# Wide probability tiles of an attention kernel normalised on ScalarE in place of VectorE

## The chip, the cores and the metric

One core of a Trainium2 chip runs the whole program. The metric is the device time of one execution in microseconds (us), lower is better. The kernel is written instruction by instruction: every engine has its own program, and the engines meet only at semaphores.

## The reference

A transformer block on 8 sequences of 512 tokens, width 512: attention with a residual, then a mixture of experts with a residual. The attention has 16 query heads in 4 groups that share a key and value head, and adds two parts, softmax attention and a gated linear recurrence. Cut to what matters here:

```python
qs = softmax(q, axis=-1)                      # "features", over the head's 128 columns
ks = softmax(k, axis=-1)
gl = log_sigmoid(g) / 16.0                    # g is k
S  = S * exp(gl_t)[..., None] + ks_t[..., None] * v_t[..., None, :]     # scan over tokens
o_gla = einsum('bhk,bhkv->bhv', qs_t, S)
scores = einsum('bqhd,bkhd->bhqk', rope(q), rope(k)) * D ** -0.5        # causal mask
attn = softmax(scores, axis=-1)
y = einsum('bhqk,bkhd->bqhd', attn, v)
out = (0.5 * y + 0.5 * o_gla) @ Wo
```

## The kernel before, in words

The program has three phases: attention, routing with the shared expert, and the 32 experts. The change touches the attention alone.

Attention works in *units*, one for each sequence and group, 8 x 4 = 32, and a first one that only prepares. A unit (`unit(c, b, g, prepare, more)`, one such function in the program of every engine) does two things side by side. It attends the four query heads of its group, and, where `prepare` is set (31 of the 32), it prepares the next unit: the query, key and value products, the rotary embedding, the softmax features, the gates, for four blocks of 128 tokens. Head s and block s share a *head step*, s = 0 to 3, so that each unit has three switches from one head to the next.

A head's scores are cut by query rows into four tiles i = 0 to 3 of 128 rows; the causal mask leaves tile i with 128 (i + 1) columns. "The fourth tile" is i = 3 (512 columns), "the third" i = 2 (384 columns): the wide ones. Each goes this way:

- TensorE, `scores` (L781, L783): the scores into `score_ps`.
- VectorE, `row_max` (L583), then ScalarE, `exponent` (L412): the exponential into `prob[:, i % 2]`, with its row sums.
- VectorE, `normalise`: the reciprocal of the row sums (L589, it counts up `inv_sum_ready`) and the multiplication in place (L591, it counts up `prob_ready`).
- TensorE, `turn_probs` (L797): waits for `prob_ready` and transposes the tile block by block. For the third tile it also waits for `o_whole_ready`, since it writes into `out_ps`, which ScalarE must have emptied.
- VectorE, `diagonal` (L599), adds the recurrence's local part to the last block; ScalarE, `past` (L418), copies the other blocks to `prob_t`.
- TensorE, `attend` (L808, L811): the products into `out_ps`. ScalarE, `out_copy` (L424, L428), empties it, GpSimd makes the low half of the output.

The features of block s: ScalarE `take_products` (L437 to L440) brings them from PSUM; VectorE `feature_max` (L605) and `rope_cosines` (L613); ScalarE `gates` (L445, L447) and `feature_exps` (five exponentials of 128 columns with row sums, L454); VectorE `gate_logs` (L619) and `soften_keys` (reciprocal L625, multiplication L627, which counts up `soft_key_ready`). In the next head step TensorE's `turn_features` (L874 and on) waits for that count and transposes, then `turn_queries` (L888), and after more products `turn_softmax` (L895). ScalarE's `turned_keys` and `turned`, VectorE's `turned_low` (L634), `apply_decays` and `keep_local` (L665), and GpSimd's functions go on from there.

In group 2 of a sequence that has a successor, each head step also turns a part of the next input: ScalarE `turned_x` (L397) behind the feature exponentials, VectorE `x_low` (L565), and `turn_queries` waits for it. In group 1 VectorE takes that input's statistics.

The order on each engine is the order in which its `unit` calls these functions; nothing is rescheduled. At a switch, ScalarE exponentiates the next head's wide tiles before `gates`, and VectorE normalises them between `keep_local` and `gate_logs`:

```python
                    if c is not None and s < G - 1:      # VectorE
                        normalise(c, s + 1, 3)
                        normalise(c, s + 1, 2)
                    if prepare:
                        gate_logs(NT * ua + s)
                        soften_keys(NT * ua + s)
```

The first head's wide tiles are normalised at the start of the unit, ahead of the steps, while TensorE runs the first query and value products.

Of the kernel before, what the change touches and what calls it, by code (L numbers as in the profile page):

```python
# [6 lines left out]
P = 128  # L7
# [6 lines left out]
ACT = mybir.ActivationFunctionType  # L14
# [6 lines left out]
G = HEADS // KV  # L21
# [3 lines left out]
NT = SEQ // P  # L25
# [16 lines left out]
def attention_phase(nc, x, w_q, w_k, w_v, w_o, consts, x2, acc, rows):  # L42
# [3 lines left out]
    with ExitStack() as ctx:  # L46
        def sb(name, shape, dt=F32):
            return ctx.enter_context(nc.sbuf_tensor(name, shape, dt))

        def sem(name):  # L50
            return ctx.enter_context(nc.semaphore(name))
# [40 lines left out]
        prob = sb("prob", [P, 2, SEQ])  # L92
# [3 lines left out]
        inv_sum = sb("inv_sum", [P, G * NT])  # L96
# [67 lines left out]
        exp_ready = [sem(f"exp_ready{n}") for n in range(2)]  # L164
        inv_sum_ready = sem("inv_sum_ready")
        prob_ready = sem("prob_ready")
        prob_turned = [sem(f"prob_turned{n}") for n in range(2)]
        past_copied = sem("past_copied")
        diag_ready = sem("diag_ready")
# [49 lines left out]
        def block_index(c, h, i):  # L219
            return G * NT * c + NT * h + NT - 1 - i  # L220

        def use_index(c, h, i):

            return G * NT // 2 * c + NT // 2 * h + (NT - 1 - i) // 2
# [152 lines left out]
        def _(act):  # L377
# [30 lines left out]
            def exponent(c, h, i):  # L408
                n, k, j, w = block_index(c, h, i), use_index(c, h, i), NT * h + i, P * (i + 1)
                act.wait_ge(max_ready, n + 1)  # L410
                act.wait_ge(prob_turned[i % 2], k)
                nc.scalar.activation(prob[:, i % 2, 0:w], score_ps[i % 2][:, 0:w], ACT.Exp, bias=neg_max[:, j:j + 1],  # L412
                                     accum_out=row_sum[:, j:j + 1]).then_inc(exp_ready[i % 2], 1)

            def past(c, h, i):
                act.wait_ge(diag_ready, block_index(c, h, i) + 1)
                act.wait_ge(attended, G * c + h)
                nc.scalar.copy(prob_t[:, 0:i, i * P:(i + 1) * P],  # L418
                               prob_ps[i % 2][:, 0:i * P].rearrange("p (j t) -> p j t", t=P)).then_inc(past_copied, 1)
# [22 lines left out]
            def gates(a):  # L442

                act.wait_ge(logs_step, 3 * a + 1)
                nc.scalar.activation(logs[:], logs[:], ACT.Exp, scale=-1.0).then_inc(logs_step, 1)  # L445
                act.wait_ge(logs_step, 3 * a + 2)
                nc.scalar.activation(logs[:], logs[:], ACT.Ln, bias=1.0).then_inc(logs_step, 1)  # L447

            def feature_exps(a, ua, i):
                act.wait_ge(tops_ready, a + 1)  # L450
                act.wait_ge(soft_turned, a)
                act.wait_ge(k_rest_ready, (NT - 1) * ua + min(i, NT - 1))
                for h in range(G + 1):
                    ins = nc.scalar.activation(soft[:, h * DH:(h + 1) * DH], qk[:, h * DH:(h + 1) * DH], ACT.Exp,  # L454
                                               bias=neg_top[:, h:h + 1], accum_out=tot[:, h:h + 1])
                ins.then_inc(exps_ready, 1)
# [19 lines left out]
            def unit(c, b, g, prepare, more):  # L476
                ua, p = (0, 0) if c is None else (c + 1, (g + 1) % 2)
                if prepare and c is not None:
                    act.wait_ge(attended, G * c)
                if c is not None:  # L480
                    exponent(c, 0, 3)
                    exponent(c, 0, 2)
                for s in range(NT):
                    if c is not None:
                        past(c, s, 3)
                        exponent(c, s, 1)
                    if prepare and s:
                        turned_keys(NT * ua + s - 1, p, s - 1)
                    if c is not None:
                        past(c, s, 2)  # L490
                        exponent(c, s, 0)
                    if prepare and s:
                        turned(NT * ua + s - 1, ua, p, s - 1)
                    if prepare:
                        take_products(NT * ua + s, p, s)
                    if c is not None:
                        if s < G - 1:
                            exponent(c, s + 1, 3)
                        past(c, s, 1)
                        if s < G - 1:  # L500
                            exponent(c, s + 1, 2)
                    if prepare:
                        gates(NT * ua + s)
                        feature_exps(NT * ua + s, ua, s)
                    if more and g == KV - 2:
                        turned_x(b + 1, s, tr_ps[min(s, 1)])
                    if c is not None:
                        out_copy(c, s, NT * ua + s if prepare else None)
                    else:
                        split_high(STAGES + s)  # L510
                if prepare:
                    turned_keys(NT * ua + NT - 1, p, NT - 1)
                    turned(NT * ua + NT - 1, ua, p, NT - 1)
                if more and g == KV - 3:
                    root(b + 1)
                if c is None:
                    act.wait_ge(w_low, STAGES + DC)
            each_sequence(act, head, unit)

        @block.vector  # L520
        def _(dve):
# [64 lines left out]
            def normalise(c, h, i):  # L586
                n, j, w = block_index(c, h, i), NT * h + i, P * (i + 1)
                dve.wait_ge(exp_ready[i % 2], use_index(c, h, i) + 1)
                nc.vector.reciprocal(inv_sum[:, j:j + 1], row_sum[:, j:j + 1]).then_inc(inv_sum_ready, 1)  # L589
                dve.wait_ge(inv_sum_ready, n + 1)  # L590
                nc.vector.tensor_scalar(prob[:, i % 2, 0:w], prob[:, i % 2, 0:w], inv_sum[:, j:j + 1], None,  # L591
                                        ALU.mult).then_inc(prob_ready, 1)
# [152 lines left out]
        def _(pe):  # L745
# [38 lines left out]
                                 stop=True).then_inc(scores_done, 1)  # L784

            def turn_probs(c, h, i):
                n = block_index(c, h, i)
                pe.wait_ge(prob_ready, n + 1)
                if i == NT - 1 and h == 0:
                    pe.wait_ge(x2_added[1], NT // 2 * c)  # L790
                if i == 2:
                    pe.wait_ge(o_whole_ready, G * c + h)
                else:

                    pe.wait_ge(past_copied, (NT - 1) * (G * c + h) + max(NT - 2 - i, 0))
                for j in range(i + 1):
                    ins = nc.tensor.transpose(prob_ps[i % 2][:, j * P:(j + 1) * P], prob[:, i % 2, j * P:(j + 1) * P], ident[:])  # L797
                ins.then_inc(prob_turned[i % 2], 1)
# [1236 lines left out]
```

## Time and profile before

| | |
|---|---|
| three runs | 2785.82, 2787.27, 2788.97 us |
| their median | 2787.27 us |
| the profiled execution's own time | 2786.35 us |
| its span, first to last instruction | 2784.3 us |
| mean granted TensorE clock over the span | 0.974 |

All durations come from the profiled execution. Its span leaves out the 2.05 us around the first and last instruction. In the rows "PE" is TensorE's matmul, "PEld" its weight load, which overlaps the matmuls, "DVE" VectorE, "ACT" ScalarE, "POOL" GpSimd, "SP" the engine that issues transfers. A row of a timeline has the start in us from the span's beginning, the duration in us, engine, line of the kernel, operation, output<-input with partitions x elements, and in brackets the idle time of the engine before it with what ended it ("issue": nothing that the profile shows). Neighbours on an engine overlap a little. The granted clock is 1.00 at TensorE's full 2.4 GHz.

### The profile page before, as it was taken

Reading aid. Unit: us, or ns where it says so; the run is one execution under the profiler, and the core shown is the slowest. Engines: PE = TensorE matmul, PEld = TensorE weight load, DVE = VectorE, ACT = ScalarE, POOL = GpSimd, SP = SyncE. Lnnn points to the kernel's source line nnn. Section 1 sums busy time; section 2 is a strip of 40 time slices with the busy share of each in tenths; the row PEclk is TensorE's granted clock in tenths of the full one; section 3 lists DMA queues with packets and bytes.
Section 4 is the critical chain, followed back from the end, with each engine's and each line's share of the span. In section 5 each row is a group of like instructions: output and inputs, shape, how many; then the busy total and the mean of one; then the engine's idle time right before and its main releaser. Section 6 shows DMA issues by size and latency. Waiting matters only on the chain. (4 is left out here: it accounts for less than half of the span.)

```text
span 2784.3 us, 52836 instructions
## 1 busy us (share of the span) xinstructions
PE 2533.7 (91%) x16740; PEld 1726.4 (62%) x16740; DVE 1912.5 (69%) x4603; ACT 1571.3 (56%) x4783; POOL 1563.6 (56%) x2010
## 2 busy tenths in 40 slices
PE   3899999999999999999999999999986899979882
PEld 2566666666666666666666666666654345457661
DVE  5777767777777776777677767777756677647661
ACT  4666556666665666666566655666644243146661
POOL 3556545655665565566556555655531666646563
PEclk9899999999999999999999999999998999989996
DMA  4500000000000000000000000000003314159985
GB/s 174 191 1 16 1 31 1 16 31 1 2 16 31 1 16 29 4 1 17 31 1 1 16 31 1 1 31 1 1 1 115 113 52 148 63 153 260 272 224 149
DMA packets 65358, 156.80 MB, mean 56 GB/s; under 512 B 13367, under 2 KB 14647, under 8 KB 64256
## 3 DMA queue, kind: packets, MB, share of 16 engines
q1 hardware_dynamic: 48624, 132.91, 14.0%
q0 software_dynamic: 16384, 16.33, 3.2%
q10 hardware_dynamic: 80, 4.19, 0.4%
q8 instruction: 141, 2.31, 0.3%
q14 instruction: 129, 1.06, 0.1%
HBM read 120.31 MB, written 81.40 MB: 72 GB/s over the span
## 5 line engine op out<-in xcount | busy, mean ns | idle before, releaser
L284 POOL TENSOR_TENSOR parts<-qk,rope 128x640 f32<-128x640 f32 x128 | 197.0, 1539 | 451.6 <-issue 303.4
L412 ACT ACTIVATE prob<-score_ps,neg_max 128x512 f32<-128x512 f32 (+3 forms) x512 | 271.8, 531 | 249.8 <-DVE neg_max L583 213.5
L808 PE MATMUL out_ps<-prob_t,val 128*128 128x512 f32 (+3 forms) x1024 | 309.0, 445 | 14.3 <-ACT prob_t L418 10.3
L781 PE MATMUL score_ps<-kr_t,qr_t 128*128 128x512 f16 (+3 forms) x1536 | 284.8, 300 | 13.2 <-ACT prob L412 11.4
L591 DVE TENSOR_SCALAR prob<-prob,inv_sum 128x512 f32<-128x512 f32 (+3 forms) x512 | 272.9, 533 | 18.0
L808 PEld LDWEIGHTS out_ps<-prob_t,val 128*128 128x128 f32 x1024 | 186.7, 192 | 135.8 <-issue 64.3
L583 DVE TENSOR_REDUCE neg_max<-score_ps 128x1 f32<-128x512 f32 (+3 forms) x512 | 237.5, 483 | 26.2 <-PE score_ps L783 20.1
L454 ACT ACTIVATE soft<-qk,neg_top 128x128 f32<-128x128 f32 x640 | 247.1, 387 | 0.8
L324 POOL TENSOR_TENSOR k_dec<-decay,keys 128x32 f32<-128x32 f32 (+3 forms) x512 | 165.0, 354 | 83.1 <-ACT decay L474 83.1
L854 PE MATMUL qkv_ps<-wq_high,x_t_high 128*128 128x512 f16 x512 | 197.0, 385 | 15.8 <-DVE wkv_low L531 15.8
L296 POOL TENSOR_TENSOR rot<-parts 128x320 f32<-128x320 f32 x128 | 110.6, 864 | 168.0 <-DVE parts L613 168.0
L589 DVE RECIPROCAL inv_sum<-row_sum 128x1 f32<-128x1 f32 x512 | 81.4, 159 | 174.4 <-ACT prob L412 174.2
L854 PE MATMUL qkv_ps<-wq_low,x_t_high 128*128 128x512 f16 x512 | 196.3, 383 | 0.0
L854 PE MATMUL qkv_ps<-wq_high,x_t_low 128*128 128x512 f16 x512 | 195.8, 382 | 0.0
L337 POOL TENSOR_TENSOR o_t_low<-parts,o_t_high 128x512 f16<-128x512 f32 x128 | 148.0, 1156 | 77.3 <-ACT parts L428 77.3
L781 PEld LDWEIGHTS score_ps<-kr_t,qr_t 128*128 128x128 f16 x1536 | 135.7, 98 | 83.0 <-ACT prob L412 38.5
L302 POOL TENSOR_TENSOR soft<-soft,inv_tot 128x512 f32<-128x512 f32 x128 | 145.9, 1140 | 63.4 <-DVE inv_tot L625 63.4
L437 ACT ACTIVATE qk<-qkv_ps 128x640 f32<-128x640 f32 x128 | 90.0, 703 | 152.8 <-issue 138.1
L1799 POOL DMA_INDIRECT acc<-e_yo,e_goal x64 | 115.1, 1799 | 106.1 <-issue 88.9
L418 ACT COPY prob_t<-prob_ps 128x384 f32<-128x384 f32 (+1 forms) x256 | 94.3, 368 | 118.0 <-DVE prob_t L599 116.4
L1257 POOL DMA_INDIRECT rows<-r_yn,r_sk_i x128 | 129.0, 1008 | 53.9 <-issue 47.3
L313 POOL TENSOR_TENSOR decay<-keys 128x512 f32<-128x512 f32 x128 | 142.5, 1113 | 6.2 <-ACT keys L461 4.2
(285 smaller groups left out, 7780.0 us busy)
## 6 DMA issues: line engine op xcount, KB each, us to landing
held_expert_w<-in_L_ffn_W_gate_dram SPq DMA_DIRECT2D x32, 512.0 KB
held_expert_w<-in_L_ffn_W_up_dram SPq DMA_DIRECT2D x32, 512.0 KB
held_expert_w<-in_L_ffn_W_down_dram SPq DMA_DIRECT2D x32, 512.0 KB, 7.2
rows<-const_empty_dram SPq DMA_DIRECT2D x1, 10560.0 KB, 39.2
e_xg<-rows SPq DMA_DIRECT2D x32, 330.0 KB
x_in<-_attn_hidden_states_dram SPq DMA_DIRECT2D x8, 1024.0 KB, 5.4
x_acc<-_attn_hidden_states_dram SPq DMA_DIRECT2D x8, 1024.0 KB, 5.4
x<-x_acc SPq DMA_DIRECT2D x8, 1024.0 KB, 4.4
```

Source lines behind the costliest of these rows:

```text
L284: nc.gpsimd.tensor_tensor(parts[:, 1, :].rearrange("p (h d) -> p h d", d=HALF), qk[:].rearrange("p (h d) -> p h d", d=HALF), rope[:, i, 1: ...
L302: nc.gpsimd.tensor_tensor(q, q, inv_tot[:, 0:G].unsqueeze(2).to_broadcast([P, G, DH]), ALU.mult).then_inc(soft_query_ready, 1)
L313: nc.gpsimd.tensor_tensor(decay[:, 0:NSUB * P].rearrange("p (c s) -> p c s", s=P), mid.to_broadcast([P, NSUB, P]), run.unsqueeze(1).to_bro ...
L324: ins = nc.gpsimd.tensor_tensor(k_dec[:, s, 0:m], decay[:, s * P:s * P + m], keys[:, 0:m], ALU.mult)
L337: nc.gpsimd.tensor_tensor(o_t[1][:, h, :], o_whole, o_t[0][:, h, :], ALU.subtract).then_inc(o_t_ready, 1)
L412: nc.scalar.activation(prob[:, i % 2, 0:w], score_ps[i % 2][:, 0:w], ACT.Exp, bias=neg_max[:, j:j + 1], accum_out=row_sum[:, j:j + 1]).the ...
L454: ins = nc.scalar.activation(soft[:, h * DH:(h + 1) * DH], qk[:, h * DH:(h + 1) * DH], ACT.Exp, bias=neg_top[:, h:h + 1], accum_out=tot[:, ...
L583: nc.vector.tensor_reduce(neg_max[:, j:j + 1], score_ps[i % 2][:, 0:w], AX_X, ALU.max, negate=True).then_inc(max_ready, 1)
L591: nc.vector.tensor_scalar(prob[:, i % 2, 0:w], prob[:, i % 2, 0:w], inv_sum[:, j:j + 1], None, ALU.mult).then_inc(prob_ready, 1)
L781: nc.tensor.matmul(score_ps[i % 2][:, 0:w], qr_t[p][:, q_, h, i * P:(i + 1) * P], kr_t[p][:, k_, 0:w], start=(n == 0), stop=False)
L808: nc.tensor.matmul(out_ps[:, j * P:SEQ], val[p][:, j, :], prob_t[:, j, j * P:SEQ], start=(j == 0), stop=False, skip_group_check=True)
L854: ins = nc.tensor.matmul(qkv_ps[:, 0:G * DH], x_t[x_part][:, d, i * P:(i + 1) * P], wq[w][:, d, gn * G * DH:(gn + 1) * G * DH], start=(d = ...
```

## The change

The two wide tiles of each head are no longer multiplied by VectorE but by ScalarE, with a Copy whose scale is the column of reciprocals (`normalise_wide`). VectorE still takes all reciprocals and multiplies the two narrow tiles. ScalarE does the fourth tile's Copy after `gates` and ahead of `feature_exps`, and the third tile's behind `feature_exps`; at a unit's start both come behind the two exponentials. The wide Copies count up a semaphore of their own, `wide_prob_ready`, for which TensorE's transposes of those tiles wait; both counts are taken per head, two for each. The instructions of TensorE, GpSimd and the transfers stay as they are, in the same order.

```diff
--- before.py
+++ after.py
@@ -164,6 +164,7 @@
         exp_ready = [sem(f"exp_ready{n}") for n in range(2)]
         inv_sum_ready = sem("inv_sum_ready")
         prob_ready = sem("prob_ready")
+        wide_prob_ready = sem("wide_prob_ready")
         prob_turned = [sem(f"prob_turned{n}") for n in range(2)]
         past_copied = sem("past_copied")
         diag_ready = sem("diag_ready")
@@ -412,6 +413,12 @@
                 nc.scalar.activation(prob[:, i % 2, 0:w], score_ps[i % 2][:, 0:w], ACT.Exp, bias=neg_max[:, j:j + 1],
                                      accum_out=row_sum[:, j:j + 1]).then_inc(exp_ready[i % 2], 1)
 
+            def normalise_wide(c, h, i):
+                n, j, w = block_index(c, h, i), NT * h + i, P * (i + 1)
+                act.wait_ge(inv_sum_ready, n + 1)
+                nc.scalar.activation(prob[:, i % 2, 0:w], prob[:, i % 2, 0:w], ACT.Copy,
+                                     scale=inv_sum[:, j:j + 1]).then_inc(wide_prob_ready, 1)
+
             def past(c, h, i):
                 act.wait_ge(diag_ready, block_index(c, h, i) + 1)
                 act.wait_ge(attended, G * c + h)
@@ -480,6 +487,8 @@
                 if c is not None:
                     exponent(c, 0, 3)
                     exponent(c, 0, 2)
+                    normalise_wide(c, 0, 3)
+                    normalise_wide(c, 0, 2)
                 for s in range(NT):
                     if c is not None:
                         past(c, s, 3)
@@ -501,7 +510,12 @@
                             exponent(c, s + 1, 2)
                     if prepare:
                         gates(NT * ua + s)
+                    if c is not None and s < G - 1:
+                        normalise_wide(c, s + 1, 3)
+                    if prepare:
                         feature_exps(NT * ua + s, ua, s)
+                    if c is not None and s < G - 1:
+                        normalise_wide(c, s + 1, 2)
                     if more and g == KV - 2:
                         turned_x(b + 1, s, tr_ps[min(s, 1)])
                     if c is not None:
@@ -587,6 +601,8 @@
                 n, j, w = block_index(c, h, i), NT * h + i, P * (i + 1)
                 dve.wait_ge(exp_ready[i % 2], use_index(c, h, i) + 1)
                 nc.vector.reciprocal(inv_sum[:, j:j + 1], row_sum[:, j:j + 1]).then_inc(inv_sum_ready, 1)
+                if i >= 2:
+                    return
                 dve.wait_ge(inv_sum_ready, n + 1)
                 nc.vector.tensor_scalar(prob[:, i % 2, 0:w], prob[:, i % 2, 0:w], inv_sum[:, j:j + 1], None,
                                         ALU.mult).then_inc(prob_ready, 1)
@@ -784,8 +800,10 @@
                                  stop=True).then_inc(scores_done, 1)
 
             def turn_probs(c, h, i):
-                n = block_index(c, h, i)
-                pe.wait_ge(prob_ready, n + 1)
+                if i >= 2:
+                    pe.wait_ge(wide_prob_ready, 2 * (G * c + h) + NT - i)
+                else:
+                    pe.wait_ge(prob_ready, 2 * (G * c + h) + 2 - i)
                 if i == NT - 1 and h == 0:
                     pe.wait_ge(x2_added[1], NT // 2 * c)
                 if i == 2:
```

How the order moves at a switch, on ScalarE, before (from the next head's third tile's exponential to the two copies of this head's output; `tot` are the row sums):

```order
L412 ACTIVATE prob,row_sum<-score_ps,neg_max 128x384 [waits prob_turned0,max_ready]
L445 ACTIVATE logs<-logs 128x128 [waits logs_step]
L447 ACTIVATE logs<-logs 128x128 [waits logs_step]
L454 ACTIVATE soft,tot<-qk,neg_top 128x128 [waits k_rest_ready,soft_turned,tops_ready]
L454 ACTIVATE soft,tot<-qk,neg_top 128x128 x4
L424 ACTIVATE o_t_high<-out_ps 128x512 [waits projected,attended]
L428 ACTIVATE parts<-out_ps 128x512 [waits rot_ready,o_t_ready]
```

and with the change, where L413 is the same exponential, L419 the new Copy, L461 the feature exponentials, L431 and L435 the output copies:

```order
L413 ACTIVATE prob,row_sum<-score_ps,neg_max 128x384 [waits prob_turned0,max_ready]
L452 ACTIVATE logs<-logs 128x128 [waits logs_step]
L454 ACTIVATE logs<-logs 128x128 [waits logs_step]
L419 ACTIVATE prob<-prob,inv_sum 128x512 [waits inv_sum_ready]
L461 ACTIVATE soft,tot<-qk,neg_top 128x128 [waits k_rest_ready,soft_turned,tops_ready]
L461 ACTIVATE soft,tot<-qk,neg_top 128x128 x4
L419 ACTIVATE prob<-prob,inv_sum 128x384 [waits inv_sum_ready]
L431 ACTIVATE o_t_high<-out_ps 128x512 [waits projected,attended]
L435 ACTIVATE parts<-out_ps 128x512 [waits rot_ready,o_t_ready]
```

Two Copies have come in, one on either side of the five feature exponentials; each waits for `inv_sum_ready`, which VectorE counts up.

VectorE at the first switch of a unit, before (from the rotary cosines to the softened keys):

```order
L613 TENSOR_TENSOR parts<-qk,rope 128x640 [waits rot_ready,o_t_ready]
L589 RECIPROCAL inv_sum<-row_sum 128x1 [waits exp_ready1]
L591 TENSOR_SCALAR prob<-prob,inv_sum 128x512 [waits inv_sum_ready]
L589 RECIPROCAL inv_sum<-row_sum 128x1 [waits exp_ready0]
L591 TENSOR_SCALAR prob<-prob,inv_sum 128x384 [waits inv_sum_ready]
L619 SCALAR_TENSOR_TENSOR gate<-qk,logs 128x128 [waits keys_turned,logs_step]
L625 RECIPROCAL inv_tot<-tot 128x5 [waits soft_query_ready,exps_ready]
L627 TENSOR_TENSOR soft<-soft,inv_tot 128x128 [waits inv_ready]
```

and with the change (L603 the reciprocals of the row sums, L635 the gate, L641 and L643 the keys):

```order
L629 TENSOR_TENSOR parts<-qk,rope 128x640 [waits rot_ready,o_t_ready]
L603 RECIPROCAL inv_sum<-row_sum 128x1 [waits exp_ready1]
L603 RECIPROCAL inv_sum<-row_sum 128x1 [waits exp_ready0]
L635 SCALAR_TENSOR_TENSOR gate<-qk,logs 128x128 [waits keys_turned,logs_step]
L641 RECIPROCAL inv_tot<-tot 128x5 [waits soft_query_ready,exps_ready]
L643 TENSOR_TENSOR soft<-soft,inv_tot 128x128 [waits inv_ready]
```

The two multiplications by `inv_sum` are gone; the two reciprocals stand next to each other, still behind what was ahead of them. At the later switches `keep_local` (L665) stands between the cosines and the reciprocals, in both kernels.

## Rows read from the trace of the kernel before

**Rows 1.** Busy time, share of the span and instructions of each engine, whole program.
```profile
PE 2533.7 (91%) x16740; PEld 1726.4 (62%) x16740; DVE 1912.5 (69%) x4603; ACT 1571.3 (56%) x4783; POOL 1563.6 (56%) x2010
```

**Rows 2.** Busy us by engine (instructions), clock, DMA share, GB/s, 64 us of attention.
```profile
1000.00:1064.00 64.00, 63.24 (x414) 43.73 (x413) 45.97 (x116) 41.44 (x141) 38.89 (x50) 1.00 0.06 18
```

**Rows 3.** Waits of TensorE: engine, line, releaser: us in total, times, longest.
```profile
PE tr_ps L874 <- DVE soft L627: 32.7, 79, 5.2
...
PEld tr_ps L874 <- issue: 33.1, 83, 0.5
```

**Rows 4.** Timeline of TensorE's weight loads, one head step.
```profile
1194.20 0.14 PEld L874 LDWEIGHTS tr_ps<-ident,rot 128*128 128x128 f32 x1 [0.38 <-issue]
...
1207.25 0.14 PEld L874 LDWEIGHTS tr_ps<-ident,rot 128*128 128x128 f32 x1 [0.37 <-issue]
...
1208.30 0.36 PEld L797 LDWEIGHTS out_ps<-ident,prob 128*128 128x128 f32 x3
```

**Rows 5.** Timeline of VectorE in the same head step.
```profile
1201.38 1.16 DVE L583 TENSOR_REDUCE neg_max<-score_ps 128x1 f32<-128x512 f32 x2 [0.36 <-PE score_ps L783]
...
1204.91 0.15 DVE L589 RECIPROCAL inv_sum<-row_sum 128x1 f32<-128x1 f32 x1
1205.09 0.52 DVE L591 TENSOR_SCALAR prob<-prob,inv_sum 128x512 f32<-128x512 f32 x1
...
1205.72 0.83 DVE L591 TENSOR_SCALAR prob<-prob,inv_sum 128x384 f32<-128x384 f32 x1
...
1206.67 0.18 DVE L625 RECIPROCAL inv_tot<-tot 128x5 f32<-128x5 f32 x1
1206.89 0.29 DVE L627 TENSOR_TENSOR soft<-soft,inv_tot 128x128 f32<-128x128 f32 x1
```

**Rows 6.** Timeline of ScalarE in the same head step.
```profile
1204.16 0.39 ACT L454 ACTIVATE soft<-qk,neg_top 128x128 f32<-128x128 f32 x1
...
1205.99 0.19 ACT L454 ACTIVATION_READ_ACCUMULATOR soft<-qk,neg_top 128x1 f32 x1
1206.32 0.60 ACT L424 ACTIVATE o_t_high<-out_ps 128x512 f16<-128x512 f32 x1
1206.82 0.59 ACT L428 ACTIVATE parts<-out_ps 128x512 f32<-128x512 f32 x1
```

**Rows 7.** ScalarE groups by shape: busy us, mean ns of one, idle before.
```profile
L418 ACT COPY prob_t<-prob_ps 128x384 f32<-128x384 f32 x128 | 61.3, 479 | 112.5 <-DVE prob_t L599 110.9
...
L1840 ACT ACTIVATE e_yo<-e_down_ps,e_share 80x512 f32<-80x512 f32 x64 | 40.8, 678 | 87.1 <-POOL e_goal L1790 79.2 <-PE e_down_ps L1940 5.7 <-DMA acc<-e_yo,e_goal 2.1
...
L1295 ACT ACTIVATE r_yn<-r_xr,r_shift,r_rstd 128x512 f32<-128x512 f32 x32 | 23.4, 805 | 7.5 <-DVE r_shift L1513 7.5
L1328 ACT CAST r_h_high<-r_h 128x512 f16<-128x512 f32 x32 | 20.2, 630 | 60.6 <-DVE r_h L1623 57.8 <-issue 2.8
```

**Rows 8.** Timeline, first switch of a group 0: ScalarE and TensorE's weight load.
```profile
1371.33 0.60 ACT L424 ACTIVATE o_t_high<-out_ps 128x512 f16<-128x512 f32 x1 [1.83 <-PE out_ps L811]
...
1371.89 0.14 PEld L874 LDWEIGHTS tr_ps<-ident,rot 128*128 128x128 f32 x1
```

**Rows 9.** Timeline, a group 2 switch, with the next input's turn.
```profile
1001.71 0.15 DVE L589 RECIPROCAL inv_sum<-row_sum 128x1 f32<-128x1 f32 x1
...
1002.89 0.58 ACT L397 ACTIVATE x_t_high<-tr_ps 128x512 f16<-128x512 f32 x1
...
1003.90 0.68 DVE L565 SCALAR_TENSOR_TENSOR x_t_low<-tr_ps,x_t_high 128x512 f16<-128x512 f32 x1
...
1004.67 0.48 PEld L888 LDWEIGHTS tr_ps<-ident,rot 128*128 128x128 f32 x4
```

**Rows 10.** Timeline, starts of a group 2 and of a group 3 unit.
```profile
1231.95 0.20 ACT L412 ACTIVATION_READ_ACCUMULATOR prob<-score_ps,neg_max 128x1 f32 x1
...
1232.80 0.47 PEld L797 LDWEIGHTS prob_ps<-ident,prob 128*128 128x128 f32 x4
...
1294.40 0.42 DVE L591 TENSOR_SCALAR prob<-prob,inv_sum 128x384 f32<-128x384 f32 x1
```

## The prediction

> **What bounds the kernel now.** I read the page first. TensorE is busy for 91% of the span, ScalarE for 56%, VectorE for 69% [rows 1]. That says where to look and not what the change is worth, so the stage comes next: 64 us of attention in the middle of the program hold 63.24 us of matmuls at a granted clock of 1.00 [rows 2]. TensorE is the bound there, and only work that makes TensorE wait can move the time. The waits in front of it are small and tell what stands close behind. The first transpose of a block's features, L874, waits for the softened keys of VectorE's L627 (32.7 us in 79 waits), and its weight load for 33.1 us in 83 more waits that end in "issue" [rows 3]. These are two views of one stop and not two sums.
>
> The timeline of one head step shows the chain behind it. The same transpose starts at 1194.20 and at 1207.25, so a step takes 13.05 us [rows 4]. The second one comes behind 0.37 us of idle. On VectorE, from the two row maxima at 1201.38 to L627 at 1206.89, one instruction follows the other with no idle [rows 5]. L627 ends at 1207.18 and L874 starts 0.07 later. Ahead of it ScalarE's five feature exponentials (L454) run from 1204.16 to 1206.18, the end of their last accumulator read [rows 6]; they are done 0.49 us before VectorE turns to them at 1206.67. So VectorE's chain decides by half a microsecond, and ScalarE's is next.
>
> **The change, part by part.**
>
> *Removed from VectorE.* In a head step the two wide multiplications stand at 1205.09 (0.52) and 1205.72 (0.83) [rows 5]. Taking both out frees about 1.2 us between the first reciprocal and the gate. If nothing else followed, the transpose would lose its 0.37 us wait and no more, since TensorE has its own work up to there. That is the most that can be won.
>
> *Added to ScalarE, and its cost.* No row shows this operation (Copy, SBUF to SBUF, scale from a column). From below: the 128x512 cast from SBUF with no column operand takes 630 ns. From above: L1295, SBUF to SBUF with two column operands, takes 805 ns. One column costs about 0.09 us by L1840, 678 ns, against L428, the same width without a column, 0.59 [rows 6, 7]; so I take 0.71 us for the fourth tile. L418 with 384 elements takes 479 ns, 0.11 less than L428 with 512, so 0.60 for the third. Neighbours on ScalarE start about 0.10 us before the end of the one ahead (1206.32 and 0.60, next at 1206.82 [rows 6]), so they hold the queue for 0.61 and 0.50. The Trainium skill, "ScalarE: Activation LUTs", section "What ACT_TABLE_LOAD costs", gives 186 + 93 + 0.833 x 512 = 706 ns as an estimate for it; the sum would be the same.
>
> *The new wait.* ScalarE now stops behind L447 until VectorE has written the reciprocal. That reciprocal is still behind L665, at 1204.91 [rows 5], and the next VectorE instruction uses it 0.19 later, so ScalarE can start at 1205.10. Before, the exponentials started at 1204.16. Queued behind the waiting instruction are the exponentials, then the third tile's Copy, then both copies of the head's output.
>
> *The sum for a step.* Exponentials start at 1205.10 + 0.61 = 1205.71, 1.55 later than before. Their last read ends 2.02 later at 1207.73. VectorE, which has been idle, takes the reciprocal (L625) at 1207.77; L627 follows 0.22 later for 0.29 us and ends at 1208.28; L874 starts at 1208.35 instead of 1207.25. **TensorE loses 1.10 us in the step**. All that follows in the step hangs on TensorE: the next row maxima wait 0.36 us for L783 [rows 5], so nothing catches up.
>
> *How many steps.* 8 sequences of 4 groups are 32 units, of which 31 prepare the next one; each has three switches from one head to the next, 93. At the first switch of a group 0 the transpose (1371.89) has no wait in front and ScalarE idles 1.83 us for the output at 1371.33 [rows 8]: 1.0 us later is hidden there, in 8 units. That leaves 85 steps: 85 x 1.10 = 93.5 us.
>
> *Units that turn the next sequence's input* (group 2, 7 of 8, 21 switches) pay more. There ScalarE's L397 (1002.89) and VectorE's L565 (1003.90, ends 1004.58) come behind the exponentials, and TensorE's L888 waits for them (1004.67) [rows 9]. Now: reciprocal 1001.71, Copy 1001.90, exponentials 1002.51 to 1004.53, third tile's Copy from 1004.43, L397 1004.93 to 1005.51, L565 ends 1006.23, L888 at 1006.30. That is 1.63 late, 0.53 more than the 1.10: 21 x 0.53 = 11.1 us.
>
> *Third tile's Copy and the output copies.* They end 1.7 us late: L428 would end at 1208.63 + 0.59 = 1209.22. The third tile's transposes (1208.30 before [rows 4]) now want them at 1209.40, so this is covered by a little; the residue further on, through L418, L412 and L634 to L895, I put at 3 us in all (from 0 to 0.2 us a step: 0 to 17).
>
> *At a unit's start* both tiles are normalised under the query products. The tightest start that I read is that of a group 2: the exponentials' last read begins at 1231.95, so the Copy runs from 1232.05 to 1232.76, and the transposes start at 1232.80 [rows 10]. So the cost is nothing; 0.1 us too much in each of 31 units would be 3 us.
>
> Sum: 93.5 + 11.1 + 3 = 107.6. The profiled execution took 2786.35 us (span 2784.3), 0.9 under the median. **Forecast: 2894 us.**
>
> **A rule to weigh.** VectorE multiplies the fourth tile in 0.52 us and the third in 0.42 to 0.83 [rows 5, 10]; ScalarE would take 0.71 and 0.60. The Trainium skill, "Perfetto Trace Analysis", section "Optimizing Scalar/DVE Operations", says that such work is faster on VectorE where it has a performance mode, but that offloading it may make sense if VectorE is saturated. By the trace the first half holds for the fourth tile alone, and for 5.8 us of a step VectorE is saturated as the rule wants, which would make the change a gain: the first rival.
>
> **Rivals.**
> 1. *The relief of VectorE reaches TensorE* (faster). This needs the exponentials to end before about 1206.7, hence a ScalarE that is not held by the reciprocal. It gives back the idle in front of L874, 33.1 us: 2753. For it: VectorE's queue has no gap. Against it: the exponentials have 0.49 us to spare and lose 1.55. It decides from a delay under 0.49 us. Chance 0.05.
> 2. *ScalarE's idle time hides it* (no change, 2786): it is idle 44% of the span [rows 1]. But in front of the exponentials and in front of L424, 0.14 us later than their end [rows 6], it has next to none. Chance 0.03.
> 3. *Half hidden*: waits later in the step, such as the 0.36 us before the row maxima, shrink, because the work that they wait for does not need the whole delay. 0.6 us a step, 51 + 6: 2843. Chance 0.12.
> 4. *ScalarE becomes the loop*: the output copies and the third tile's transposes add their own lateness to the first. 1.7 us for each of 85 steps, 145 us: 2931. For it: 1.7 us late against 1.1 covered only by the third tile's place in TensorE's order. Chance 0.12.
>
> **The numbers.** The main case has 0.68. Its own ends: with 0.63 and 0.81 us for the Copy the step is 1.02 to 1.20, so 87 + 0 to 102 + 16 + 17, that is 2873 to 2921. The range reaches into both slower neighbours: 2857 to 2930, which leaves out the first two rivals and the outer half of each of the other two. About 0.2% (5.6 us) is what a measurement can tell from no change. Faster 0.05, same 0.03, slower 0.92.
>
> **What would show it.** ScalarE's wide Copy at 0.71 us, idle in front of it released by the reciprocal, about 0.8 us in most steps; the exponentials followed at once by L625 and L627; waits of TensorE on L627 near 1.5 us in 85 steps, 100 us more in all; head steps of 14.15 us; VectorE with 1.3 us less work a step and more idle, and a granted clock still 1.00. The forecast is wrong if the reciprocals run earlier than after L665, if the step grows by more than 1.3 us (then the output copies are it), or if L874 waits as before.

## The result and the profile after

| | before | after |
|---|---|---|
| median of the runs on one chip | 2786.55 us (4 runs, 2784.80 to 2788.97) | 2899.62 us (4 runs, 2898.39 to 2900.48) |
| profiled execution, span | 2786.35, 2784.3 us | 2899.02, 2896.9 us |
| mean granted clock | 0.974 | 0.974 |

The ratio is 1.0405 with a 95% interval of 1.0387 to 1.0423: slower, by 113 us. The forecast was 2894 us, in a range of 2857 to 2930, with 0.92 on slower.

The page of the changed kernel, busy time of each engine, beside [rows 1]:

```profile
PE 2545.6 (88%) x16740; PEld 1733.2 (60%) x16740; DVE 1753.2 (61%) x4347; ACT 1705.3 (59%) x5039; POOL 1554.3 (54%) x2010
```

VectorE has lost 159 us of work and ScalarE has gained 134 us, so the change did what it says. TensorE has 12 us more busy time in a span 112.6 us longer. It hardly works longer, it waits. The same unit, one of group 3, before and after (stretch, its length, busy us of PE, PEld, DVE, ACT and POOL with instructions, clock, DMA share, GB/s):

```profile
1282.68:1344.34 61.66, 60.84 (x401) 42.30 (x400) 44.55 (x110) 38.51 (x132) 34.52 (x48) 1.00 0.03 11
1355.78:1420.75 64.97, 60.84 (x401) 42.26 (x400) 39.17 (x102) 42.53 (x140) 34.32 (x48) 1.00 0.03 10
```

The matmuls are the same 60.84 us, and the unit is 3.31 us longer.

Where it waits is in the chain of stops before the transposes of a block's features, `turn_features`, now L892 (L874 in [rows 3]). The waits of TensorE and its weight load (total us, times, longest):

```profile
PE tr_ps L892 <- issue: 108.1, 86, 1.4
PE tr_ps L892 <- DVE x_t_low L579: 14.4, 7, 2.1
...
PEld tr_ps L892 <- issue: 125.2, 86, 1.6
PEld tr_ps L892 <- DVE x_t_low L579: 16.0, 7, 2.3
```

The weight load's 33.1 us in 83 waits before [rows 3] are 125.2 in 86 now. The forecast was 85 steps at near 1.5 us each, 100 us more; it is 92.1 us more. ScalarE's groups by shape (busy us, mean ns of one, idle before):

```profile
L419 ACT ACTIVATE prob<-prob,inv_sum 128x512 f32<-128x512 f32 x128 | 92.2, 721 | 77.7 <-DVE inv_sum L603 77.7
L419 ACT ACTIVATE prob<-prob,inv_sum 128x384 f32<-128x384 f32 x128 | 76.9, 601 | 0.0
```

The Copies take 0.72 and 0.60 us (0.71 and 0.60 were taken), and 77.7 us are spent in front of the fourth tile's, in 94 waits, waiting for the reciprocal. No wait stands in front of the third tile's.

One head step after, the one that answers to [rows 4 to 6]. TensorE's weight loads:

```profile
1246.78 0.14 PEld L892 LDWEIGHTS tr_ps<-ident,rot 128*128 128x128 f32 x1 [1.58 <-issue]
...
1260.93 0.14 PEld L892 LDWEIGHTS tr_ps<-ident,rot 128*128 128x128 f32 x1 [1.48 <-issue]
```

VectorE:

```profile
1256.88 0.68 DVE L681 SCALAR_TENSOR_TENSOR local<-tr_ps,keep 128x512 f32<-128x512 f32 x1
1257.48 0.21 DVE L603 RECIPROCAL inv_sum<-row_sum 128x1 f32<-128x1 f32 x2
1257.62 0.44 DVE L635 SCALAR_TENSOR_TENSOR gate<-qk,logs 128x128 f32<-128x128 f32 x1
1260.35 0.19 DVE L641 RECIPROCAL inv_tot<-tot 128x5 f32<-128x5 f32 x1 [2.29 <-ACT soft L461]
1260.57 0.29 DVE L643 TENSOR_TENSOR soft<-soft,inv_tot 128x128 f32<-128x128 f32 x1
```

ScalarE:

```profile
1256.52 0.31 ACT L454 ACTIVATE logs<-logs 128x128 f32<-128x128 f32 x1
1257.67 0.72 ACT L419 ACTIVATE prob<-prob,inv_sum 128x512 f32<-128x512 f32 x1 [0.84 <-DVE inv_sum L603]
1258.30 0.39 ACT L461 ACTIVATE soft<-qk,neg_top 128x128 f32<-128x128 f32 x1
...
1260.13 0.19 ACT L461 ACTIVATION_READ_ACCUMULATOR soft<-qk,neg_top 128x1 f32 x1
1260.22 0.60 ACT L419 ACTIVATE prob<-prob,inv_sum 128x384 f32<-128x384 f32 x1
```

Read together: ScalarE is done with the gates at 1256.83 and stands until VectorE, behind `keep_local`, has written the reciprocal. The Copy starts at 1257.67, the exponentials 0.63 later, and their last read ends at 1260.32. VectorE has been idle for 2.29 us by then. It takes `soften_keys` at once and ends at 1260.86, and TensorE starts 0.07 later. The step is 14.15 us, where it was 13.05. VectorE, the engine that was relieved, stands idle for the engine that was loaded.

The trace gives the length of all 31 units that prepare another, from the last `turn_features` of the unit ahead to the last of this one. Before and after, in us, by kind of unit:

| unit | number | before | after | change of all |
|---|---|---|---|---|
| groups 1, 3, and 2 without a next input | 16 | 61.65 | 64.97 | +52.9 |
| group 2 with a next input | 7 | 63.28 | 68.54 (4), 70.20 (3) | +41.9 |
| group 0 | 7 | 64.58 (4), 65.80 (3) | 67.30 | +15.4 |
| the very first that attends | 1 | 63.69 | 64.84 | +1.2 |

The sum is 111.3 of the 112.6 us by which the span grew. The rest is 2.9 us more ahead of the first of these stops and 1.5 us less behind the last; the profiles of the experiments differ by such amounts there too, so it says nothing of the change.

### The profile page after: what moved, and what is told of

It reads as the page before. It is cut to its first block and busy times, and to the rows that moved or that the text cites. A ratio compares the mean times of both kernels' runs of the same rounds, so it can differ in the third digit from the quotient of the medians.

```text
span 2896.9 us, 52836 instructions
## 1 busy us (share of the span) xinstructions
PE 2545.6 (88%) x16740; PEld 1733.2 (60%) x16740; DVE 1753.2 (61%) x4347; ACT 1705.3 (59%) x5039; POOL 1554.3 (54%) x2010
## 3 DMA queue, kind: packets, MB, share of 16 engines
q14 instruction: 129, 1.06, 0.1%
## 5 line engine op out<-in xcount | busy, mean ns | idle before, releaser
L413 ACT ACTIVATE prob<-score_ps,neg_max 128x512 f32<-128x512 f32 (+3 forms) x512 | 271.5, 531 | 251.1 <-DVE neg_max L597 214.6
L461 ACT ACTIVATE soft<-qk,neg_top 128x128 f32<-128x128 f32 x640 | 246.8, 387 | 0.8
L303 POOL TENSOR_TENSOR soft<-soft,inv_tot 128x512 f32<-128x512 f32 x128 | 145.9, 1140 | 173.6 <-DVE inv_tot L641 173.6
L419 ACT ACTIVATE prob<-prob,inv_sum 128x512 f32<-128x512 f32 (+1 forms) x256 | 165.6, 661 | 77.7 <-DVE inv_sum L603 77.7
L603 DVE RECIPROCAL inv_sum<-row_sum 128x1 f32<-128x1 f32 x512 | 73.1, 158 | 217.0 <-ACT prob L413 217.0
L297 POOL TENSOR_TENSOR rot<-parts 128x320 f32<-128x320 f32 x128 | 111.3, 870 | 167.7 <-DVE parts L629 167.7
L892 PE MATMUL tr_ps<-ident,rot 128*128 128x128 f32 x128 | 38.5, 301 | 139.3 <-issue 108.1
L641 DVE RECIPROCAL inv_tot<-tot 128x5 f32<-128x5 f32 x128 | 24.1, 188 | 215.6 <-ACT soft L461 215.1
```

The lines of the kernel that those rows point to most:

```text
L303: nc.gpsimd.tensor_tensor(q, q, inv_tot[:, 0:G].unsqueeze(2).to_broadcast([P, G, DH]), ALU.mult).then_inc(soft_query_ready, 1)
L419: nc.scalar.activation(prob[:, i % 2, 0:w], prob[:, i % 2, 0:w], ACT.Copy, scale=inv_sum[:, j:j + 1]).then_inc(wide_prob_ready, 1)
```

## The experiments

Theory A was the prediction's: the reciprocal, held up in VectorE's queue, holds ScalarE's queue, and behind it the feature exponentials. Its main rival, B, was that the Copies' own time on ScalarE costs what was lost, wherever they stand. Each kernel was timed beside the kernel before on the same chip: its median there was 2783.76 us for the first four, 2786.12 for the next four, 2785.37 for two and 2786.97 for the last. "Step" is a plain head step, 13.05 us before and 14.15 after.

**1. Only the unit's start.** The change with its Copies at the start of a unit alone, and none at the three switches. Against the changed kernel:

```diff
 gates(NT * ua + s)
-normalise_wide(c, s + 1, 3)
 feature_exps(NT * ua + s, ua, s)
-normalise_wide(c, s + 1, 2)
...
-if i >= 2:
+if i >= 2 and h == 0:
     return
```

> Both wide tiles on ScalarE for the first head of each unit alone, VectorE keeps them at the three switches. Theory A (the loss is the lateness of the feature exponentials at the switches, by the wait for the reciprocal and the fourth tile's Copy ahead of them): unit starts are covered, 2786.5 us as before, within 4. Theory B (the Copies' 1.3 us of ScalarE time a head cost wherever they stand): a quarter of the loss of 113, so about 2815.

Measured: 2787.17 us, ratio 1.0008 (0.9999 to 1.0018); every step as before. The Copies at the unit's start, 64 of 256, cost nothing that the times or the steps show. They stand under the query products, as the prediction had it.

**2. The wait alone.** The kernel before, with no Copy at all, where ScalarE waits ahead of `feature_exps` as the change makes it wait:

```diff
+if c is not None and s < G - 1:
+    act.wait_ge(inv_sum_ready, block_index(c, s + 1, 3) + 1)
 feature_exps(NT * ua + s, ua, s)
```

> The kernel before with one thing more: at a switch ScalarE waits for the fourth tile's reciprocal ahead of the feature exponentials; no Copy. Theory A: exponentials 0.94 us later, of which 0.49 were spare against VectorE's chain, so the head step grows from 13.05 to about 13.5; 85 x 0.49 = 42, and some 8 more in the units that turn the next input: about 2836. Theory B: no work is added, 2787.

Measured: 2832.93 us, ratio 1.0169 (1.0151 to 1.0187), step 13.54. Its waits of ScalarE and of the weight load:

```profile
ACT soft L454 <- DVE inv_sum L591: 76.8, 93, 0.9
...
PEld tr_ps L876 <- issue: 71.2, 82, 1.0
```

76.8 us of waiting, as good as the 77.7 of the changed kernel, cost 49 us with no work added anywhere. By the prediction's chain the wait makes the exponentials 0.94 us late (1205.10 for 1204.16); in this trace they start 0.93 us later in the step. Of that 0.49 is free, which leaves 0.45; the step grew by 0.49, and the weight load waits 71.2 us for 33.1.

**3. The Copies without the wait.** The change with both reciprocals earlier in VectorE's queue, so that the Copy finds its column there:

```diff
 feature_max(NT * ua + s)
+normalise(c, s + 1, 3)
 rope_cosines(NT * ua + s, s, 0 if c is None else G * c + s)
+normalise(c, s + 1, 2)
...
-normalise(c, s + 1, 3)
-normalise(c, s + 1, 2)
```

> The changed kernel with VectorE's two reciprocals moved up, the fourth tile's behind the feature maxima, the third's behind the rotary cosines; the Copies stay. Theory A: ScalarE no longer waits, exponentials only 0.61 us later than in the kernel before, head step about 13.2; 64 x 0.16 and 21 x 1.0 in the units that turn the next input: about 2819. Theory B: same work in the same place, 2899.

Measured: 2814.72 us, ratio 1.0105 (1.0088 to 1.0122), step 13.21. Its ScalarE group and its waits:

```profile
L419 ACT ACTIVATE prob<-prob,inv_sum 128x512 f32<-128x512 f32 (+1 forms) x256 | 164.1, 655 | 0.0
```

```profile
PEld tr_ps L894 <- issue: 44.2, 84, 0.5
```

All Copies stay, no wait is in front of them, and 82 of 113 us are gone. The Copy's 0.63 us less the 0.49 that is free leaves 0.14, and the step grew by 0.16.

**4. Both Copies behind the exponentials.**

```diff
 gates(NT * ua + s)
-normalise_wide(c, s + 1, 3)
 feature_exps(NT * ua + s, ua, s)
+normalise_wide(c, s + 1, 3)
 normalise_wide(c, s + 1, 2)
```

> The changed kernel with both Copies behind the feature exponentials. Theory A: exponentials back in time, TensorE waits instead for the fourth tile, 0.8 us, and no longer 0.4 for the keys: head step about 13.5, 64 x 0.45 + 21 x 1.1 = 52, about 2839. Theory B: the same ScalarE work ahead of the output copies, 2899.

Measured: 2831.09 us, ratio 1.0167 (1.0150 to 1.0184), step 13.46. The exponentials are as early as before and the keys are ready 0.45 us earlier in the step, and the kernel still loses 47 us. TensorE's transposes of the fourth tile (`turn_probs`) stand ahead of `turn_features`, and the tile's Copy is now what they wait for. Before and here:

```profile
PEld prob_ps L797 <- DVE prob L591: 2.8, 2, 2.1
```

```profile
PEld prob_ps L814 <- ACT prob L419: 67.8, 93, 2.5
```

So the fourth tile's Copy is dear ahead of the exponentials by what it holds up, and behind them by its own lateness. The output copies and the third tile are late as well, but the third tile's transposes wait here no more than before (1.9 us in all).

**5 and 6. Each tile by itself.** The change with ScalarE taking the fourth tile alone, in its place ahead of the exponentials, and with ScalarE taking the third alone, behind them, at a unit's start too; VectorE keeps the other. The first, and then the second:

```diff
 normalise_wide(c, s + 1, 3)
 feature_exps(NT * ua + s, ua, s)
-normalise_wide(c, s + 1, 2)
...
-if i >= 2:
+if i == 3:
     return
```

```diff
-normalise_wide(c, s + 1, 3)
 feature_exps(NT * ua + s, ua, s)
 normalise_wide(c, s + 1, 2)
...
-if i >= 2:
+if i == 2:
     return
```

> Of the change the fourth tile alone: its Copy stays ahead of the feature exponentials, the third tile is VectorE's again. Theory A: plain head steps stay at 14.15, since all of the loss is in what stands ahead of the exponentials; in the units that turn the next input L397 comes 0.5 us sooner, 10 us in all: before plus 102, about 2889 where before is 2787. Theory B (every Copy on ScalarE costs by its own time): somewhat over half of the loss, before plus 61.

> Of the change the third tile alone: its Copy behind the feature exponentials, the fourth tile is VectorE's again. Theory A: nothing is put ahead of the exponentials and VectorE's chain loses 0.6 to 0.8 us, so TensorE's 0.37 us wait before its transposes of the features goes: plain head steps 12.7, 64 x -0.37 = -24; the Copy delays L397 by 0.5 us in 21 steps, +10: before minus 14. Theory B: before plus 52, slower.

Measured: 2889.27 us for the fourth tile alone, ratio 1.0369 (1.0353 to 1.0385), step 14.16. 2770.34 us for the third alone, ratio 0.9942 (0.9927 to 0.9958), step 12.78. The loss is all in one of the two Copies; the other is a gain. Together they do not simply add: with the fourth tile's wait in force the third tile's relief of VectorE can't reach TensorE, and in group 2 units its 0.5 us a step comes on top (68.54 us a unit, 67.04 with the fourth alone).

**7. The third tile's Copy behind the next input's turn as well.** Against experiment 6; the same kernel was also timed once more:

```diff
 feature_exps(NT * ua + s, ua, s)
-normalise_wide(c, s + 1, 2)
 turned_x(b + 1, s, tr_ps[min(s, 1)])
+normalise_wide(c, s + 1, 2)
```

> As the kernel with the third tile alone, but in the units that turn the next input the Copy stands behind L397. Theory A: the 21 steps lose their 10 us penalty: before minus 24, ratio 0.991. Theory B: before plus 52.

> The kernel with the third tile alone behind L397 once more, beside the last one on the same chip: before minus 18, as measured, within 3.

Measured: 2768.06 us, ratio 0.9930 (0.9916 to 0.9943), and in the repeat 2767.79, 0.9937 (0.9924 to 0.9951). This beats both kernels, but a gain of 24 us was expected and 18 were measured. Group 2 units went from 63.68 in the experiment before it to 63.17, 3.6 us for seven and not the 10 expected. The weight load and VectorE's gate in a plain step:

```profile
1184.38 0.14 PEld L889 LDWEIGHTS tr_ps<-ident,rot 128*128 128x128 f32 x1
```

```profile
1183.00 0.88 DVE L632 SCALAR_TENSOR_TENSOR gate<-qk,logs 128x128 f32<-128x128 f32 x1
1183.80 0.18 DVE L638 RECIPROCAL inv_tot<-tot 128x5 f32<-128x5 f32 x1
1184.01 0.29 DVE L640 TENSOR_TENSOR soft<-soft,inv_tot 128x128 f32<-128x128 f32 x1
```

No idle is left in front of the transpose here; in all, the 33.1 us in 83 waits of [rows 3] are 5.8 in 28. This is the first rival's gain: 0.27 us of the step's 0.37 us wait, and not more, as the prediction said of its bound. The gate now takes 0.88 us for 0.28, since it begins beside a GpSimd instruction (last section).

**8. The same gain without ScalarE (a miss).** The kernel before, where VectorE normalises the third tile behind `soften_keys`:

```diff
 normalise(c, s + 1, 3)
-normalise(c, s + 1, 2)
 gate_logs(NT * ua + s)
 soften_keys(NT * ua + s)
+normalise(c, s + 1, 2)
```

> The kernel before, with all work on VectorE, but the third tile's reciprocal and multiplication moved behind the gate and the softened keys. Theory A: the same chain is cut as by giving the tile to ScalarE, so the same -24, less what the later diagonal addition and low half of the keys give back in front of TensorE's L895, up to 0.2 us a step: before minus 10 to minus 24. Theory B (relief of VectorE counts by its work): no work has gone, before within 3.

Measured: 2818.66 us, ratio 1.0118 (1.0103 to 1.0134), 32 us slower, where a gain was expected. The keys are early, but the multiplication is only moved. In the last step of a group 0 unit, VectorE and GpSimd there:

```profile
1162.95 0.29 DVE L627 TENSOR_TENSOR soft<-soft,inv_tot 128x128 f32<-128x128 f32 x1
1163.16 0.15 DVE L589 RECIPROCAL inv_sum<-row_sum 128x1 f32<-128x1 f32 x1
1163.35 1.00 DVE L591 TENSOR_SCALAR prob<-prob,inv_sum 128x384 f32<-128x384 f32 x1
```

```profile
1162.99 1.14 POOL L302 TENSOR_TENSOR soft<-soft,inv_tot 128x512 f32<-128x512 f32 x1 [0.33 <-DVE inv_tot L625]
```

and further on TensorE's weight load for the queries' softmax:

```profile
1167.85 0.42 PEld L896 LDWEIGHTS tr_ps<-ident,soft 128*128 128x128 f32 x4 [0.57 <-DVE kr_t L634]
```

The multiplication takes 1.00 us, since it begins while GpSimd works, all that VectorE does next is late, and TensorE waits at `turn_softmax` (60.6 us in 85 waits, 5.7 in 16 before) in place of `turn_features`. The units tell where this is dear: those of group 3 take 61.75 us for 61.65, those of group 1, where VectorE also takes the next input's statistics, 63.52 to 63.74, and those of group 2 with a next input 65.43 for 63.28. So the loss lies where VectorE has more to do behind the keys.

**9. The gates behind too (a miss).** From experiment 7, the gate exponentials behind the feature exponentials on ScalarE and, on VectorE, the keys ahead of the gate:

```diff
-gates(NT * ua + s)
 feature_exps(NT * ua + s, ua, s)
 turned_x(b + 1, s, tr_ps[min(s, 1)])
+gates(NT * ua + s)
...
-gate_logs(NT * ua + s)
 soften_keys(NT * ua + s)
+gate_logs(NT * ua + s)
```

> As the kernel with the third tile alone behind L397, and ScalarE's two gate functions moved behind the feature exponentials and L397, VectorE's gate behind the softened keys: the exponentials start when the feature maxima are there, some 0.45 us sooner. Theory A (the exponentials' end is what TensorE's transposes of the features wait for): the waits that are left go, plain head steps 12.7, and the 21 steps with the next input gain up to 0.45: before minus 28, 10 under the kernel with the third tile alone. Theory C (with VectorE relieved the exponentials no longer decide): no gain over that kernel.

Measured: 2850.60 us, ratio 1.0235 (1.0221 to 1.0249), step 13.56. VectorE and GpSimd:

```profile
1229.08 0.51 DVE L640 TENSOR_TENSOR soft<-soft,inv_tot 128x128 f32<-128x128 f32 x1
1229.51 1.12 DVE L632 SCALAR_TENSOR_TENSOR gate<-qk,logs 128x128 f32<-128x128 f32 x1
```

```profile
1228.38 1.05 POOL L298 TENSOR_TENSOR rot<-parts 128x320 f32<-128x320 f32 x1
1229.39 1.09 POOL L303 TENSOR_TENSOR soft<-soft,inv_tot 128x512 f32<-128x512 f32 x1
```

The keys are ready at 1229.59, but the gate, for which the transposes also wait, takes 1.12 us. The reciprocal of the keys (L638) releases GpSimd's L303, and the gate comes while it runs.

**10. Only that undone.** Experiment 9 with VectorE's gate ahead of the keys again:

```diff
-soften_keys(NT * ua + s)
 gate_logs(NT * ua + s)
+soften_keys(NT * ua + s)
```

> As e9_gates_behind on ScalarE (the gate exponentials behind the feature exponentials and turned_x), but VectorE makes the gate ahead of soften_keys again, as the kernel before does. If e9 lost its time because its gate on VectorE ran beside the GpSimd multiplication that the reciprocal ahead of it releases, the gate is back at 0.3 to 0.9 us here and TensorE's plain head step is 12.8 to 13.1 us instead of 13.56: 2765 to 2795 us. The rival, that the gate exponentials are late by themselves once they stand behind the two other groups on ScalarE, keeps the step near 13.5 and the time near 2850 us, with VectorE's gate waiting for ScalarE's logs rather than running long.

Measured: 2784.51 us, ratio 0.9994 (0.9984 to 1.0003), step 12.89. VectorE's gate there:

```profile
1180.24 0.30 DVE L632 SCALAR_TENSOR_TENSOR gate<-qk,logs 128x128 f32<-128x128 f32 x1 [0.62 <-ACT logs L454]
```

VectorE's order alone gave back 66 us, and the gate is at its short time again. What is left of experiment 9's edit, the late gate exponentials, for which VectorE now waits 0.62 us, makes it 16 us slower than experiment 7: a plain unit takes 61.15 us for 60.86 (16 units, 5 us) and a group 2 unit with a next input 64.48 for 63.16 (7 units, 9 us).

## Why the prediction was right

*The bound.* TensorE's stop at `turn_features` decided, as read from [rows 2 to 6]. 111.3 of 112.6 us lie between these stops.

*The Copy.* Taken as 0.71 and 0.60 us between neighbours of [rows 6, 7]; 721 and 601 ns measured.

*The new wait and the step.* The chain of the prediction, from 1205.10 to 1208.35, came out within 0.02 us at every link: Copy to exponentials 0.63 for 0.61, exponentials 2.02, keys 0.54 after their end, transpose 0.07. The step grew by 1.10 us, as forecast. Experiments 2 and 3 split it. The wait alone costs 0.49, the Copy alone 0.16, and both together not 0.65 but 1.10, because the 0.49 us that the exponentials had to spare is free only once. 0.94 of wait and 0.63 of Copy, less 0.49, is 1.08.

*How many steps.* 85 x 1.10 = 93.5 was right for the 16 plain units: 52.8 forecast, 52.9 measured. In group 0, with its first switch held to be hidden, 17.6 was forecast for 8 units, the very first among them. In fact the first switch grew by 0.51 us (26.33 to 26.84): ScalarE's idle time in [rows 8] was no full cover. Three of these units lost only 1.50 us in place of 2.71, since a fall of the clock that the kernel before has there is gone (below). The very first unit grew by only 1.2 us: its two plain steps by 1.10 each, while its first, in which the clock is low for 12.5 us before and for 9.3 after, shrank by 1.06. So the group's sum came to 16.5, and that it is near 17.6 is luck.

*Units that turn the next input.* This term was mis-sized: 21 x 0.53 was too little. The three switches and what follows them went from 23.99, 13.05, 13.62 and 12.62 to 25.65, 14.15, 15.42 and 13.31. That is 5.25 us a unit where 4.9 was forecast, and 1.66 us more in three of the seven. 34.2 us was forecast for them, 41.9 measured. The nothing at a unit's start held (experiment 1); the 3 us put down for the third tile's residue are not to be seen in plain steps, which grew alike with and without its Copy (experiment 5). The total was 107.6 against 112.6. The 7.7 us by which this term was short are more than that difference: the 3 us for nothing and the 1.1 of group 0 made up for a part, and that much of the closeness is luck.

*A slip in it.* The output copies were said to end 1.7 us late; by the prediction's own times it is 1209.22 less 1207.41, 1.81, and 1.79 was measured. At 1.81 a step the fourth rival would have stood at 2940 us. The sum does not use it, and the cover that it was held against (1209.40) was there.

*The rivals.* The first, relief of VectorE, is real once ScalarE is not held: experiments 6 and 7 gain 16 and 18 us by it. The prediction's condition, exponentials delayed by less than 0.49 us, is what separates them from the change. The second, ScalarE's idle time, falls to experiment 2: with no work added, 49 us are lost. The third, half hidden, falls to the step. The fourth, ScalarE as the loop, falls to the step and to experiment 5: without the third tile's Copy all but 10 us of the loss is still there.

*The rule weighed.* VectorE had no gap in the 5.8 us ahead of the transpose, and the rule of the Trainium skill ("Perfetto Trace Analysis", section "Optimizing Scalar/DVE Operations") would have made the offload a gain. Of the third tile that held (0.993), of the fourth it did not (1.037). What decides is where in the receiving engine's queue the work stands and what it waits for.

## What to carry to other kernels

Work that is given to another engine brings its wait along: look at what is queued behind it there, compare the wait with how early that work is now, and subtract the slack once for wait and work together. Here the tile whose Copy stood behind the urgent work could be given away at a gain. The one whose input came from the busy engine at the last moment lost in its place ahead of that work, and also with its input made earlier (experiment 3) and, together with the other, behind it (experiment 4); alone behind it, it was not tried. When something is moved on VectorE, see which GpSimd instruction will run beside it in its new place.

## What the hardware showed

*VectorE behind GpSimd.* The gate has both inputs in SBUF. In the step of [rows 5] GpSimd is done at 1206.34 and the gate takes

```profile
1206.47 0.28 DVE L619 SCALAR_TENSOR_TENSOR gate<-qk,logs 128x128 f32<-128x128 f32 x1
```

Begun while a GpSimd TENSOR_TENSOR ran, it ended 0.15 us behind that instruction's end: 1183.88 in experiment 7 against 1183.73, 1230.63 against 1229.39 + 1.09 in experiment 9. So did the keys (1229.59 against 1228.38 + 1.05). The 128x384 multiplication, 0.42 us alone [rows 10], took 0.83 in [rows 5] and 1.00 in experiment 8, 0.22 behind GpSimd's end. It is a stop until the other is done, not a slower pace: all 128 gates of experiment 9 began beside GpSimd, took 0.75 to 1.12 us and ended 0.15 behind it. Instructions with an input in PSUM keep their time: the diagonal (L599) takes 0.28 us beside GpSimd and without it. The Trainium skill, "SBUF — State Buffer", section "Who interferes with whom", says that VectorE with two SBUF inputs or in a two-port mode and GpSimd block each other for a whole instruction; the runs agree, for GpSimd too: its second half of the rotary sum (L297) takes 1.05 us where VectorE multiplies the fourth tile just ahead of it and 0.91 to 0.92 in the changed kernel and in experiments 3 and 4, where it does not. It also means that the 0.83 us freed in the step was half waiting.

*The clock after a long wait.* In three of seven group 2 units the clock fell behind the longest of the new waits. The changed kernel in stretches of 2 us (busy us by engine, granted clock, DMA share, GB/s):

```profile
1043.00:1045.00 2.00, 0.40 (x5) 0.16 (x2) 0.77 (x3) 2.00 (x7) 1.00 (x1) 1.00 0.00 0
1045.00:1047.00 2.00, 1.54 (x8) 1.54 (x9) 1.28 (x5) 1.72 (x6) 1.42 (x3) 0.68 0.00 0
1047.00:1049.00 2.00, 2.00 (x13) 1.66 (x12) 0.69 (x3) 0.73 (x3) 2.00 (x1) 0.50 0.03 8
```

TensorE was busy for 0.40 of 2 us, and then the clock was at its lower level of 1.2 GHz for some 3 us; it cost 1.66 us. The four other units, with the same waits, kept 1.00. The kernel before had this in three of seven group 0 units:

```profile
1110.00:1112.00 2.00, 0.88 (x4) 0.31 (x4) 0.92 (x4) 1.18 (x6) 0.00 (x0) 1.00 0.34 102
...
1114.00:1116.00 2.00, 1.89 (x3) 0.86 (x4) 1.97 (x4) 1.97 (x10) 0.74 (x2) 0.57 0.07 26
1116.00:1118.00 2.00, 2.00 (x7) 1.28 (x6) 1.93 (x6) 1.09 (x6) 1.40 (x3) 0.58 0.00 0
```

There each cost 1.22 us (65.80 against 64.58), and they are gone after. Three drops went and three came, +5.0 and -3.7 us, so in these fourteen units the clock took 1.3 us of the 113. The prediction had expected it at 1.00 throughout. Among the experiments such drops come and go: the profile of experiment 6 has none in these units, those of experiment 7 and of its repeat have three of 1.5 us in group 0. Why one unit has a drop and its like has none stays open.
